# A decoder layer on one core: row maxima handed to the score products as three bfloat16 parts in six rows, and penalty rows loaded earlier

## The reference, cut to what matters

```python
x = _layernorm(x + self_attn(x))       # 1024 tokens, 16 heads of width 8, one K and V head shared by all
x = _layernorm(x + cross_attn(x, ctx)) # 6404 context rows, a mask of 1024 x 6404, 16 K and V heads
x = _layernorm(x + ffn(x))             # 8 experts, the best one per token

# both attentions, per head:
scores = einsum('qd,kd->qk', Q, K) / sqrt(8)      # cross: -1e9 where mask == 0
attn = softmax(scores)                            # softmax subtracts the row's maximum
out = attn @ V
```

## Time and profile before

| what | value |
|---|---|
| median of 3 runs | 467.17 us (465.81 to 469.11) |
| the profiled execution | 469.97 us, its span on the core 467.7 us |
| granted TensorE clock, mean | 0.974 of full speed |
| busy: PE, DVE, ACT, POOL | 94%, 85%, 77%, 52% of the span |
| PE matmul records | 3885 |

### The profile page before, as it was taken

How to read it: one execution, slowest core, us unless ns; L and a number is a source line. 1 busy time by engine, 2 the same in 40 slices (tenths; PEclk the granted TensorE clock), 3 DMA queues, 4 the chain that set the end, 5 groups by cost and what they waited for, 6 DMA issues and landing times.

```text
span 467.7 us, 10803 instructions
## 1 busy us (share of the span) xinstructions
PE 440.9 (94%) x3885; PEld 176.7 (38%) x3887; DVE 396.7 (85%) x522; ACT 358.4 (77%) x704; POOL 245.1 (52%) x381
## 2 busy tenths in 40 slices
PE   8999999999899999799999999999999999999983
PEld 2433333333334443233343334333443443333441
DVE  4989999999699689689998999999999999941455
ACT  6328889688677877588968988889868788878723
POOL 4726879976799604122447644444447254320453
PEclk9889999999899999989999999999999999999978
DMA  5849968679680073211232346322212122110000
GB/s 129 322 115 315 283 218 297 264 263 332 228 329 13 3 135 80 65 45 46 84 90 69 101 93 111 92 60 58 88 51 70 39 81 69 47 29 26 5 22 25
DMA packets 24595, 56.07 MB, mean 120 GB/s; under 512 B 6442, under 2 KB 15928, under 8 KB 22492
## 3 DMA queue, kind: packets, MB, share of 16 engines
q0 software_dynamic: 7536, 37.91, 24.6%
q1 hardware_dynamic: 16424, 17.24, 14.1%
q10 hardware_dynamic: 580, 0.20, 0.2%
HBM read 45.60 MB, written 9.18 MB: 117 GB/s over the span
## 4 chain that ended last, share of the span: by engine, by line
PE 76%; DVE 10%; DMA 5%; issue 4%; ACT 2%; POOL 2%; POOLq 0%; DVEq 0%; ACTq 0%
PE O L1503 29%; PE ST L1739 15%; PE ST L1530 9%; PE RT L1732 7%; DVE mxs L935 6%; DMA Qs<-mxr 5%; PE RT L1518 4%; PE RT L1625 2%; PE ST L1632 2%; PE RT L1429 1%; PE O L1481 1%; ACT prob L1302 1%; PE RT L1587 1%; PE RT L1595 1%; DVE mxc L952 1%
## 5 line engine op out<-in xcount | busy, mean ns | idle before, releaser
L1302 ACT ACTIVATE prob<-ST 128x512 f32<-128x512 f32 x512 | 279.5, 599 | 59.0 <-PE ST L1530 29.3
L935 DVE TENSOR_REDUCE mxs<-RT 128x2 f32<-128x1024 f32 x128 | 153.0, 1222 | 14.6 <-PE RT L1518 13.5
L952 DVE TENSOR_REDUCE mxc<-RT 128x2 f32<-128x1024 f32 x128 | 152.8, 1221 | 5.8 <-PE RT L1732 5.4
L1739 PE MATMUL ST<-Qs,Kc 64*128 64x512 f32 x320 | 117.4, 450 | 0.0
L1732 PE MATMUL RT<-Kr,Qs 64*128 64x512 f32 (+1 forms) x384 | 114.4, 400 | 2.1 <-issue 2.1
L1503 PE MATMUL O<-prob,vst 128*9 128x256 f32 x1280 | 99.1, 381 | 1.7 <-ACT prob L1291 0.5
L1530 PE MATMUL ST<-Qs,Kself 64*128 64x512 f32 x256 | 96.7, 449 | 4.0 <-DMA Qs<-mxr 3.8
L1518 PE MATMUL RT<-Kself,Qs 64*128 64x512 f32 x256 | 89.3, 465 | 2.2 <-DVE Kself L912 0.9
L681 POOL DMA_DIRECT2D Kr<-kd x96 | 47.8, 502 | 75.9 <-PE RT L1732 60.8
L1503 PE MATMUL O<-prob,Vs 128*9 128x256 f32 x1024 | 81.0, 388 | 1.2 <-ACT osb L1246 0.3
L1739 PEld LDWEIGHTS ST<-Qs,Kc 64*128 64x128 f32 x320 | 50.5, 184 | 65.8 <-issue 38.7
(11 more groups left out here) (219 smaller groups left out, 327.4 us busy)
## 6 DMA issues: line engine op xcount, KB each, us to landing
big<-in_mask POOLq DMA_DIRECT2D x16, 1664.0 KB, 7.3
Kc<-kd POOLq DMA_DIRECT2D x64, 80.0 KB, 2.2
Kr<-kd POOLq DMA_DIRECT2D x64, 64.0 KB, 2.1
od_s<-osb SPq DMA_DIRECT2D x16, 128.0 KB, 2.5
kd<-Vx SPq DMA_DIRECT2D x4, 512.0 KB, 6.9
Qs<-qd_x SPq DMA_DIRECT2D x8, 256.0 KB
od_x<-osb SPq DMA_DIRECT2D x14, 128.0 KB, 1.7
Qs<-qd_s SPq DMA_DIRECT2D x12, 128.0 KB, 5.9
```

The costliest lines, as they stand in the source:

```text
L935: freed(v.tensor_reduce(mxs[:, h % 2, c2, :].rearrange("p (f t) -> p f t", f=2)[:, :, q], bank[:, :].rearrange("p (f k) -> p f k", f=2), A ...
L952: return v.tensor_reduce(o[:, :, u % 4], src, AX.X, ALU.max)
L1302: freed(nc.scalar.activation(prob[:, s % SLOTS, f * HALF:(f + 1) * HALF], bank[:, :], ACT.Exp))
L1739: mm = mmul(o[:, :], Kc[STACK[f], b * P:(b + 1) * P], Qs[STACK[f], j, :], start=True, stop=not gen, skip_group_check=True)
```

## The change

The stacks of 64 rows are laid out anew: the products begin at partitions 0 and 96 in place of 1 and 67, and the maxima lie in six rows, 36 to 86 in steps of 10, three for each head, in place of four rows. The maximum is cut into three bfloat16 parts, so that `split_max` has four operations, each waiting for the one before, where it had two. The turn is a bfloat16 matmul of 24 columns against a bfloat16 identity (`identb`, made once on POOL at the start), where it was a float32 one of 16 columns. The DMA from `mxr` to `Qs` moves 24 rows of 512 bytes for 16. The load that clears the maximum rows for the second phase of queries has another shape. The penalty loads are issued on SP straight after the penalties' stores, at h = 13, ahead of the next maxima and of the chunk's stores, in place of after them.

```diff
-PRODUCTS = (1, 64 + 3)
-MAXROWS = slice(0, 100, 33)
+PRODUCTS = (0, 96)
+MAXROWS = slice(36, 87, 10)
...
-        mxh = sb("mxh", [P, 2, 2, 4], F32R)
-        mxr = sb("mxr", [16, 2, P])
+        mxl = sb("mxl", [P, 2, 4])
+        mxh = sb("mxh", [P, 2, 3, 4], BF16)
+        identb = sb("identb", [P, P], BF16)
+        mxr = sb("mxr", [24, 2, P])
...
-                load(Qs[MAXROWS, 8 * ph:8 * ph + 8, :].bitcast(F32).rearrange("o h q -> o (h q)"), zerof[:, :], "xq_in")
+                load(Qs[MAXROWS, 8 * ph:8 * ph + 8, :].bitcast(F32).rearrange("o h (t q) -> o (h t) q", q=P),
+                     zerof[0:6, :].unsqueeze(1).to_broadcast([6, 32, P]), "xq_in")
...
-                if h == 14:
-                    more_keys()
                     sp.wait_ge(S("pen_out"), 16 * 5)
                     sp.wait_ge(S("k_clean"), 2)
                     for k_ in (Kr, Kc):
                         load(k_[PENROWS[0]:PENROWS[1] + 1:PENROWS[1] - PENROWS[0], :].bitcast(F32),
                              pd.to_broadcast([2, KUSE]), "pen_in")
+                if h == 14:
+                    more_keys()
...
+            pool.wait_ge(S("cst"), 1)
+            g_.tensor_copy(identb[:, :], ident[:, :]).then_inc(S("identb_made"), 1)
...
-                g_.tensor_copy(mxh[:, :, 0, :], parts).then_inc(S("mx_part"), 1)
+                step(g_.tensor_copy(mxh[:, :, 0, :], parts))
+                step(g_.tensor_tensor(mxl[:, :, :], parts, mxh[:, :, 0, :], ALU.subtract))
+                g_.tensor_copy(mxh[:, :, 1, :], mxl[:, :, :]).then_inc(S("mx_part"), 1)
                 pool.wait_ge(S("mx_part"), G + 1)
-                g_.tensor_tensor(mxh[:, :, 1, :], parts, mxh[:, :, 0, :].bitcast(F32), ALU.subtract) \
+                g_.tensor_tensor(mxh[:, :, 2, :], mxl[:, :, :], mxh[:, :, 1, :], ALU.subtract) \
                     .then_inc(S("mx_split"), 1)
...
-                rows = mxh[:, :, :, :].bitcast(F32).rearrange("p f k t -> p (f k t)")
-                if bank is None:
-                    mm = mmul(O[0:16, 256:256 + P], rows, ident[:, :], start=False, stop=False, skip_group_check=True)
-                else:
-                    mm = nc.tensor.transpose(ST[bank][0:16, 0:P], rows, ident[:, :])
+                if G == 0:
+                    pe.wait_ge(S("identb_made"), 1)
+                o = O[0:24, 256:256 + P] if bank is None else ST[bank][0:24, 0:P]
+                mm = mmul(o, mxh[:, :, :, :].rearrange("p f k t -> p (f k t)"), identb[:, :], start=bank is not None,
+                          stop=bank is not None, skip_group_check=True)
```

More of the change, by code:

```diff
@@ L262, in decoder_layer @@
             "ctx_in kd_out kd_more k_clean vx_ones kr0 kr1 kr2 kc0 kc1 vs0 vs1 mx_folded x_bias bias_tile dve_chain "
-            "rt_ready rt_free st_ready st_free pv mx mx_part mx_split mx_turned mx_copied max_in0 max_in1 "
+            "rt_ready rt_free st_ready st_free pv mx mx_part mx_split mx_turned identb_made mx_copied max_in0 max_in1 "
             "o_copied o_in0 o_in1 o_back o_last den_in rden var std xn xq_high xq_low xq_out xq_in "
@@ L880, in _ @@
                 mark(v.tensor_reduce(rowc[:, f, 1:2], ident[:, r + 2 * DH:r + PROD], AX.X, ALU.add))
-                mark(v.tensor_tensor(rowc[:, f, 2:3], ident[:, 66 * f:66 * f + 1], ident[:, 66 * f + 33:66 * f + 34],
-                                     ALU.add))
+                r = MAXROWS.start + 3 * MAXROWS.step * f
+                mark(v.tensor_reduce(rowc[:, f, 2:3], ident[:, r:r + 21:10], AX.X, ALU.add))
                 mark(v.tensor_reduce(rowc[:, f, 3:4], parts[:, :, 0, :], AX.XY, ALU.add))
@@ L1236, in max_copy @@
                     act.wait_ge(S(f"max_in{G % 2}"), 16 * (G // 2))
-                turned = O[0:16, 256:256 + P] if bank is None else ST[bank][0:16, 0:P]
+                turned = O[0:24, 256:256 + P] if bank is None else ST[bank][0:24, 0:P]
                 nc.scalar.copy(mxr[:, G % 2, :], turned).then_inc(S("mx_copied"), 1)
```

## The result

| | median of 21 runs | ratio, with its 95% interval |
|---|---|---|
| before | 469.05 us (465.81 to 471.48) | 1 |
| after | 466.06 us (463.04 to 475.28) | 0.9944 (0.9924 to 0.9964) |

The change gains 2.6 us (1.7 to 3.6), where 4.3 were forecast: on the 467.17 us that the forecast started from, 464.6 for 462.9. A second measurement gave 0.9932 (0.9894 to 0.997), 3.2 us.

The account below looks back on a forecast made before the run. PE, busy 440.9 of 467.7 us, was taken as the bound. The terms 2.9 + 1.5 + 0.6 - 0.3 - 0.4 = 4.3 us off 467.17 gave 462.9 us, with an 8-in-10 range of 459.5 to 466.8.

Parts of the forecast that it names:

- Bound and penalty loads: PE bounds the kernel; its 2.06 us wait before row 128 is for the penalty loads, and moving them gains 2.9 us.
- Turn 15: After the early penalty loads, PE waits about 1.4 us at turn 15 for POOL's split, leaving 2.9 of 4.0 us gained.
- rival E: The 2.06 us wait before row 128 was for xq_in or kr0 and stays; gain 1.4, 465.8 us; chance 0.04.
- rival B: The clock falls anyway, in the new wait at turn 15, losing 1.2 us again; 464.1 us; chance 0.12.
- ten tight turns: Turns whose weight load follows the split by only 0.32 to 0.34 us; they gain 0.06 to 0.08 each, 0.6 together.
- four with room: From the ten turns with split margins of 1.2 us or more, counted at 0.15 us each, 1.5 for all ten.
- Rival A: Splits grow by 0.3 or less, tight turns gain fully, turns 4 to 8 count; 7.1 us gained, 460.1; chance 0.22.
- rival D: Slower: POOL's split becomes PE's bound; gain used up at 0.92 us of split growth, 470.8 us at 1.2; chance 0.06.
- One turn: One bfloat16 pass for two float32 passes on PE saves 0.15 to 0.16 us of a turn's 0.20.
- Turns 9 and 10: Turn 9 had just enough room to gain 0.15 us; turn 10, already waiting 0.76 for POOL, loses 0.4.
- turns 0 to 8: Up to 1.2 us gained in PE's stream, counted as 0 because the wait for unit 8's maxima grows instead.
- Rival C: The 24-piece maxima DMA takes longer under mask loads; unit 8's wait grows 1 to 3 us; about 465; chance 0.14.

Follow-up runs that it names:

- experiment 2: Kernel before with only the two penalty loads moved early; ratio 0.9899 to the kernel before, 4.7 us less.
- experiment 7: Changed kernel with split 15 put ahead of POOL's wait for the chunk's keys; ratio 0.9945 to the kernel before.
- experiment 6: Kernel before with a bfloat16 turn of two parts, 16 rows and a two-operation split; ratio 0.9934, 3.1 us less.
- experiment 11: Kernel before with early penalty loads and a two-part bfloat16 turn, short split, 16 pieces; ratio 0.9855, 6.8 us less.
- experiment 3: Changed kernel with the penalty loads put back behind the chunk's stores; ratio 1.0012 to the kernel before.
- 12: Kernel before with early penalty loads, profiled a second time with no edit; its tail took 55.2 us for 53.6.
- experiment 4: Kernel before with two more dependent operations in each split, results unread, turn still float32; ratio 1.0056, 2.6 us more.
- 5: Kernel before with the new stacks and six maxima rows alone, float32 turn, two-operation split, late penalty loads; ratio 1.0013.
- 9: Kernel before with six maxima rows (24 pieces) and four-operation split, float32 turn, late penalty loads; ratio 1.0114 from four executions.
- experiment 10: Changed kernel with mask load 6 issued ahead of split 4 on POOL; ratio 0.9969 to the kernel before.
- 8: Kernel before with early penalty loads and the maximum as one bfloat16 part written by DVE, no POOL split; ratio 0.986, 6.5 us less.
- 1: The changed kernel measured again without an edit; ratio 0.9932 to the kernel before.

## Why it came out so

**Bound and penalty loads: right. Turn 15: right in kind.** The 2.06 was `pen_in`; rival E is out by experiment 2. F15-16 gives 3.1 us for the forecast's 2.9. The wait left at turn 15 showed as 0.74 where I had 1.4; with the longer weight-load-to-pair time it costs 0.94 (experiment 7) for the forecast's 1.07 (200.05 - 198.98). The clock did not fall in it: rival B is out.

**Turns in cross-attention: the sum right by luck, its parts not.** F16-31 is 0.92 less; by the forecast 0.9 (ten tight 0.6, four with room 0.6, turn 28 -0.3). By the landmarks the ten tight turns gave 0.08 to 0.13 a unit, 1.1 together, for 0.06 each; 0.04 of that is that the split grew by 0.53 and not 0.57. The four with room gave 0.2 together: 0.01 to 0.03 in units 18, 19 and 26, and 0.17 in unit 27, for 0.15 each. Turn 28 cost 0.4. Rival A needed splits that grow by 0.3, rival D by 0.92: both out.

**One turn: right.** With the short split (experiments 6 and 11) ten of the fifteen units from 16 to 30 are 0.13 to 0.17 shorter, for the forecast's 0.15 to 0.16, and the step with turn 21 shows the turn at 0.04 for 0.20. In units 18, 19 and 26 nothing of it arrives, so that the mean is 0.117 (F16-31 of experiment 11: 1.75 less for 15 units). The Trainium skill's 81 ns (TensorE: Matmul & The Clock Gate, section Back-to-back issue gap) made it 0.12 in the prediction. For a single turn this trace doesn't agree, it saves 0.16; that the mean comes to 0.12 as well has another reason.

**Turns 9 and 10.** Turn 10 waited 1.28 for 0.76, the 0.4 of the forecast and its shorter turn. Turn 9 was counted as having room; it waited 1.40 for split 9, and in experiment 2, with the short split, 1.26. In the kernel before the longer wait at unit 8 had hidden that.

**The step that failed: the terms at nothing before row 128.** Those counted sum to 3.1 + 0.3 + 0.9, in turns 9 to 11 0.2 more, so 4.3 to 4.5; the ratios gave 2.6 to 3.2. The prediction put turns 0 to 8 at 0, because the wait at unit 8 would absorb them, and the maxima load of 24 pieces at 0, also for the units whose loads run beside mask loads. The runs showed a wait of 1.5 to 2.6 us at unit 4 in place of none, and no gain from the parts (experiment 3). F0-9 is longer instead:

| kind of kernel, traces | F0-9 |
|---|---|
| before and experiments 2, 12: 16 pieces, short split, float32 | 95.30, 95.45, 95.61 |
| 4: long split; 5: 24 pieces; 9: both | 95.28; 95.55; 97.22 |
| 6, 11: bfloat16 turn, 16 pieces, short split | 97.14, 97.41 |
| after (second measurement), 3, 7: all three | 97.73, 99.49, 100.42 |
| 10: all three, mask load 6 earlier | 95.45 |
| 8: one part, 8 pieces, no split | 94.48 |

In the changed kernel's trace the 2.4 us are 1.0 from unit 0's maxima to unit 1's (the longer stretch at the lower clock, 19.9 to 30.1), 1.4 from unit 5's to unit 6's (the wait at unit 4), 0.5 from unit 2's to unit 5's, less 0.5 that the turns gave in units 1, 7 and 8. Experiments 6 and 11 have the first of these, and the wait at unit 3 in place of that at unit 4.

Rival C was this in kind (0.14, gain 1.3 to 3, "about 465"; measured 0.9944 of 467.17 is 464.6), but at the wrong place. It said unit 8; the wait there shrank (2.62 to 1.96). What the six rows and the long split add is at unit 4, by two causes that meet. SP's and POOL's timelines, before:

```profile
65.87 0.60 POOL L541 DMA_DIRECT2D big<-in_mask  x1
```

```profile
67.40 0.68 SPq L315 DMA_DIRECT2D Qs<-mxr  x1
```

and of experiment 3, with the wait on PE that came of it:

```profile
66.65 0.60 POOL L546 DMA_DIRECT2D big<-in_mask  x1
```

```profile
67.03 0.80 SPq L317 DMA_DIRECT2D Qs<-mxr  x1
```

```profile
75.19 0.50 PE L1537 MATMUL ST<-Qs,Kself 64*128 64x512 f32 x1 [2.56 <-DMA Qs<-mxr]
```

In these traces' DMA packets (the last 512-byte packet of each load) the maxima of unit 4 landed 6.2 to 6.6 us after POOL issued mask load 6 in the six traces with 16 pieces, whether they were issued 0.4 or 4.1 us behind it; with 24 pieces 7.1 to 7.4 in the five traces where they were issued up to 1.5 behind it (6.4 in experiment 10, 3.8 behind). That is the first cause, 0.9 us by the medians. The six-row load also has half as many bytes again, and the runs don't tell pieces from bytes. The second is POOL's order: split 4 stands ahead of mask load 6, which is issued 2.94 us after unit 4's `finx` for 2.40. In experiment 3 the load had a start of 0.4 us on the maxima for 1.5. The long split alone gives a wait of 0.8 at unit 4 and 24 pieces alone one of 1.0, without a longer F0-9; both, with the bfloat16 turn, give 1.5 to 2.6, and in two of these three executions a low clock after it: from unit 5's maxima to unit 6's took 13.8 us for 10.0. That an earlier turn asks for the maxima sooner is argued, not shown. The windows of experiment 3 after its wait have the clock at 0.67 and 0.50, where the kernel before has 1.00:

```profile
76.00:78.00 2.00, 2.00 (x20) 0.43 (x12) 1.73 (x2) 2.00 (x5) 2.00 (x1) 0.67 0.98 413
78.00:80.00 2.00, 2.00 (x16) 0.76 (x13) 1.10 (x2) 0.96 (x3) 1.92 (x2) 0.50 0.66 280
```

Experiment 10 shows the cause of the wait at unit 4 by taking it away. It also shows that POOL's order gives the time back at split 9, so no run prices unit 4 in the median by itself.

**Where the median's gain goes.** Each timed run lists span and mean granted clock. The clock records of the traces have two levels only, 0.50 and 1.00 of full speed (1.2 and 2.4 GHz). So 2 x (1 - clock) x span is the time at the lower, and the span less half of that is an estimate of what the run would take at the upper. Means:

| kernel (runs) | span | at low clock | at full clock throughout |
|---|---|---|---|
| before (26, 27, 17) | 466.2 to 466.5 | 20.3 to 21.2 | 455.9 to 456.3 |
| 2: penalty loads (6) | 461.9 | 16.3 | 453.7 |
| 6: bfloat16 turn (11) | 463.6 | 23.2 | 452.0 |
| 4: long split (12) | 469.1 | 22.5 | 457.9 |
| 5: six rows (12) | 467.0 | 22.1 | 455.9 |
| 9: long split, six rows (4) | 471.6 | 26.2 | 458.5 |
| 3: all but penalty loads (12) | 467.3 | 25.3 | 454.6 |
| the change, first measurement (20) | 463.8 | 20.4 | 453.6 |
| 1: the change (11) | 463.5 | 19.7 | 453.6 |
| 7: the change, split 15 first (8) | 463.5 | 21.2 | 452.9 |
| 10: the change, mask load 6 first (11) | 464.9 | 23.3 | 453.2 |
| 11: penalty loads, bfloat16 turn (6) | 460.3 | 17.0 | 451.8 |
| 8: one part (6) | 459.3 | 22.8 | 447.9 |

The time at the low clock scatters by 3 to 4 us from run to run, so its means are known to 1 or 2; the last column's to 0.2 to 0.7. At full clock the change stands where the penalty loads alone do (453.6 and 453.7): the bfloat16 turn takes off 3.9 us (experiment 6) and the long split adds 1.6 (experiment 4), but on top of the penalty loads the turn takes off only about 1.6 (experiments 11 and 2, each against the kernel before in its own measurement). Whether the turns of units 0 to 8 gain or are swallowed by later waits is therefore not settled. At the low clock the penalty loads alone save 4.0 us by the means, and the change 0.6: some 3.4 us come back. The parts thus cost as much as they bring, and the change earns no more than the penalty loads do.

**Left open.** The 95% intervals of 2 and 1 overlap, so the parts' net cost on top of the penalty loads (0.9899 to 0.9932) is not settled by these runs. Experiments 8 and 11 stand level in the median because 8 has 5.8 us more at the low clock, while it is 3.9 shorter at full clock. One such stretch is in its trace: PE waits 2.16 us for DVE at 133.94, and the clock is at its lower level from 134.1 to 141.0. Whether that belongs to the kernel wasn't tried. Nor was a split in three stages.

## What to carry to other kernels

A term put at nothing because "a wait there absorbs it" needs the wait's own releaser priced under the change: here it was a DMA whose length and whose rival's start both moved. A step that is made longer on a helper engine also delays every DMA that stands behind it in that engine's order. A late wait can hide another one: with the wait at unit 8 shorter, split 9 came last. And ask first how exact the value must be: what a softmax subtracts cancels between numerator and denominator, as long as every key of a query gets the same value, so that one rounded part can stand for three. With the penalty loads early that kernel took 6.5 us less than before, and the one with two parts 6.8.

## What the runs showed of the hardware

The clock falls after a wait in one execution and not after the same wait in another. At the logits of cross-attention PE waits 0.48 us in all fourteen traces (362 us in the kernel before). In three of them the clock then fell, and unit 28's maxima came 1.45 to 1.5 us later. Experiment 3's windows, and the same place before:

```profile
364.00:366.00 2.00, 1.52 (x15) 1.09 (x16) 1.98 (x3) 1.08 (x2) 0.78 (x4) 1.00 0.04 12
366.00:368.00 2.00, 2.00 (x21) 0.52 (x13) 1.70 (x8) 1.32 (x3) 0.35 (x1) 0.70 0.00 0
368.00:370.00 2.00, 2.00 (x16) 0.63 (x12) 1.18 (x2) 0.89 (x3) 0.65 (x2) 0.50 0.29 72
```

```profile
362.00:364.00 2.00, 1.52 (x18) 1.26 (x18) 1.95 (x4) 0.78 (x2) 0.06 (x1) 1.00 0.01 4
364.00:366.00 2.00, 2.00 (x22) 0.74 (x17) 1.76 (x7) 1.34 (x3) 0.70 (x2) 1.00 0.01 4
```

The tail is such a draw too: it took 51.7, 53.4 to 53.6 or 55.0 to 55.3 us in all fourteen, and 53.6 and 55.2 for one and the same program. The windows in it, of the kernel before and of the changed one:

```profile
448.00:450.00 2.00, 2.00 (x5) 1.25 (x6) 1.21 (x7) 0.23 (x1) 1.72 (x3) 0.50 0.00 0
450.00:452.00 2.00, 2.00 (x4) 0.68 (x3) 0.73 (x4) 0.00 (x0) 2.00 (x4) 0.50 0.11 33
```

```profile
443.00:445.00 2.00, 1.18 (x10) 1.00 (x10) 0.65 (x4) 0.58 (x1) 1.27 (x1) 1.00 0.00 0
445.00:447.00 2.00, 2.00 (x9) 1.18 (x9) 1.78 (x14) 0.23 (x1) 1.28 (x2) 1.00 0.03 8
```

One profile of each kernel can thus differ by 3.5 us from this alone; comparing stretches between landmarks, and leaving out those where the clock fell, gave sums that single spans would not. The 51.7 came up four times in eight traces with a bfloat16 turn and never in six without: whether that is chance is open.

In cross-attention, where no mask load is on the way, a maxima load took 1.42 to 1.49 us from issue to the end of its last piece with 16 pieces (kernel before) and 1.53 to 1.63 with 24 (changed kernel), and SP took 0.68 and 0.80 to issue one. The Trainium skill (DMA: Bandwidth & Descriptors, section Why a DMA increments its semaphore by 16 and not by 1) gives a rule for the number of engines, from which the prediction worked out that the six-row load takes no longer. On a free queue that holds to 0.1 us; close behind a mask load the six-row load landed 0.9 us later. No run here shows the engines apart.
